# Rotary and pattern attention with four PSUM banks for scores and three for everything else, where they had three and four

## The reference, cut to what matters

```python
# rotary (L0 attn_b)
q = (layernorm(x, ...) @ Wq + bq) ; k, v = ...        # 16 heads of 16
q, k = apply_rotary(q, x), apply_rotary(k, x)
qn, kn = layernorm(q, ...), layernorm(k, ...)
att = softmax(einsum('bhqd,bhkd->bhqk', qn, kn) / sqrt(16))
a = einsum('bhqk,bhkd->bhqd', att, v);  out = a @ Wo + bo
# pattern (inside L1 attn_a)
p_probs = softmax(einsum('bhqd,bhkd->bhqk', pq, pk) * 16 ** -0.5)
pattern_out = (p_probs @ pv) @ sp_o_w.T
```

## Time and profile before

| | |
|---|---|
| median of 3 runs | 4378.23 us (4376.72 to 4392.27) |
| the profiled execution | 4388.44 us, its span 4386.7 us |
| TensorE busy | 3812.8 us (87% of the span) |
| VectorE, ScalarE, GpSimd busy | 58%, 39%, 31% |
| mean granted TensorE clock | 0.933 |

### The profile page before, as it was taken

How to read it: one execution, slowest core, us unless ns; L and a number is a source line. 1 busy time by engine, 2 the same in 40 slices (tenths; PEclk the granted TensorE clock), 3 DMA queues, 4 the chain that set the end, 5 groups by cost and what they waited for, 6 DMA issues and landing times. The chain is left out here.

```text
span 4386.7 us, 45573 instructions
## 1 busy us (share of the span) xinstructions
PE 3812.8 (87%) x16352; PEld 2470.1 (56%) x16352; DVE 2547.1 (58%) x4291; ACT 1716.1 (39%) x2934; POOL 1356.8 (31%) x1074
## 2 busy tenths in 40 slices
PE   5879888887988886999998988999888888889999
PEld 3657644445754443555555546788744444367887
DVE  5655456664456665767676756433466776564333
ACT  2423255653235552333333323222256656532222
POOL 3224312213321104333333324444322221144442
PEclk8989989998989987999999998999989999989999
DMA  2000000001000002000010111000000000010000
GB/s 75 1 22 21 14 1 1 1 1 43 17 6 6 5 22 77 25 20 25 19 26 17 27 34 38 26 26 19 19 1 1 1 1 1 6 42 22 26 9 20
DMA packets 32909, 83.35 MB, mean 19 GB/s; under 512 B 6320, under 2 KB 7472, under 8 KB 32304
## 3 DMA queue, kind: packets, MB, share of 16 engines
q1 hardware_dynamic: 32688, 80.44, 6.1%
HBM read 59.44 MB, written 4.19 MB: 15 GB/s over the span
## 5 line engine op out<-in xcount | busy, mean ns | idle before, releaser
L1175 DVE TENSOR_REDUCE max_cols<-ps 128x1 fp32r<-128x512 f32 x1024 | 634.7, 681 | 219.6 <-PE ps L1105 218.7
L1150 ACT ACTIVATE probs<-ps 128x512 f32<-128x512 f32 x1024 | 549.9, 606 | 262.1 <-PE ps L1114 173.4
L768 POOL TENSOR_TENSOR h_lo<-h,h_hi 128x512 fp32r<-128x512 f32 x304 | 392.1, 1290 | 819.2 <-ACT h_hi L853 819.2
L932 DVE TENSOR_TENSOR gated<-silu,ps 128x512 f32<-128x512 f32 x288 | 198.1, 688 | 680.6 <-PE ps L235 656.5
L847 ACT ACTIVATE silu<-ps 128x512 f32<-128x512 f32 x304 | 181.6, 598 | 896.8 <-PE ps L235 896.7
L233 PE MATMUL ps<-xn_hi,w_hi 128*128 128x512 f32 x1216 | 483.1, 397 | 0.0
L234 PE MATMUL ps<-xn_lo,w_hi 128*128 128x512 f32 x1216 | 476.9, 392 | 0.0
L235 PE MATMUL ps<-xn_hi,w_lo 128*128 128x512 f32 x1216 | 476.3, 392 | 0.0
L338 POOL CAST o_hi<-o_scaled 128x512 fp32r<-128x512 f32 x64 | 39.0, 610 | 869.2 <-DVE o_scaled L1197 869.2
L1120 PE MATMUL ps<-probs,v_aug 128*32 128x512 f32 x2048 | 294.9, 650 | 0.5 <-ACT probs L1150 0.5
L1105 PE MATMUL ps<-k_alone,q_stack 128*128 128x512 f32 x512 | 215.4, 444 | 53.8 <-DVE max_cols L1175 24.9
(11 more groups left out here) (462 smaller groups left out, 7842.7 us busy)
## 6 DMA issues: line engine op xcount, KB each, us to landing
raw<-in_w_ffn SPq DMA_DIRECT2D x76, 448.0 KB, 3.2
raw<-raw SPq DMA_DIRECT2D x256, 64.0 KB, 2.0
composed_inputs<-in_m_latent SPq DMA_DIRECT2D x2, 2560.0 KB, 9.4
raw<-in_w_mamba SPq DMA_DIRECT2D x8, 448.0 KB, 5.8
raw<-in_w_latent SPq DMA_DIRECT2D x5, 448.0 KB, 6.3
x<-in_x SPq DMA_DIRECT2D x4, 512.0 KB, 6.7
gated_pattern<-gated SPq DMA_DIRECT2D x4, 512.0 KB, 3.4
raw<-gated_pattern SPq DMA_DIRECT2D x4, 512.0 KB, 4.4
```

What stands on the lines that cost most here:

```text
L768: nc.gpsimd.tensor_tensor(HL[:, b % 3, :], hb[:, b % 2, :], HH[:, b % 3, :].bitcast(F32), ALU.subtract).then_inc(G.sem, G.step((s, ev)))
L932: nc.vector.tensor_tensor(ga if routed(i) else hb[:, i % 2, :], sg[:, i % 2, :], bank[2 + i % 2], ALU.mult).then_inc(V.sem, V.step((s, "ga ...
L1150: nc.scalar.activation(self.PB[:, n % 8, :], self.scores(n), ACT.Exp, scale=self.scale).then_inc(A.sem, A.step((s, ("exp", n))))
L1175: nc.vector.tensor_reduce(self.MB[:, self.tile_of(g, h) % 2, q, col:col + 1], self.psum(ev), op=ALU.max, axis=AX.X, negate=True).then_inc( ...
```

## The change

In rotary and pattern the scores get banks 0 to 3, all other items but `pv` share banks 4, 5 and 7, and `q_stack` gets a third buffer: the same numbers as in grouped. The list of items, their order and the sizes of all instructions stay as they are.

```diff
-                self.SCORES, self.AUXB, self.NQ = ((0, 1, 2, 3), (4, 5, 7), 3) if k_tiles else ((0, 1, 2), (3, 4, 5, 7), 2)
+                self.SCORES, self.AUXB, self.NQ = ((0, 1, 2, 3), (4, 5, 7), 3) if k_tiles else ((0, 1, 2, 3), (4, 5, 7), 2)
```

## The result

The changed kernel took 4408.78 us, the median of 8 runs (4401.44 to 4416.68), against 4383.59 us for the kernel before, the median of 8 (4376.72 to 4395.70): 1.0053 of it, with an interval of 1.0037 to 1.0069. That is 0.5% slower: 25.2 us between the medians, 23 us by the ratio. I had predicted 4387 us and a range of 4362 to 4410. The profiled execution took 4411.63 us, its span 4409.7 us.

What follows compares the result with a forecast made beforehand. No engine was full; TensorE, with the longest queue, waited for exponentials and auxiliary banks. A loss of 13.5 us less 2 x 1 and 2.5 gave 9 us on a 4378 us median: 4387 us, range 4362 to 4410.

Steps and rivals of the forecast that it cites:

- rival 1: The fourth score bank pays: half of the 44 us idle before the scores comes back, 4356 us; chance 0.13.
- rival 2: In half the groups auxiliary banks bind in full, ScalarE then late for stacks' copies; 30 us, 4408; chance 0.13.
- rival 3: The clock: a tenth more of the two stages' 776 us at the lower level, 19 us, 4406; chance 0.12.
- 0.45 us a group: Loss taken as the middle of all 30 groups that carry maxima of a next group; 13.5 us.
- second step: Pattern group: maxima matmuls wait longer for banks; pv moves from 1586.20 to 1586.8, bias 0.4 us late, taken up later.
- third step: Pattern group: bias bank wanted one maxima matmul earlier; pv 0.6 us late, not covered, reaching the next group.
- The fourth stack: Pattern group: it now waits for the copy of the first stack, so its load goes 0.3 us late.
- Other groups: Groups with a value projection after the bias: pv about 0.5 us late; rotary's groups estimated at 0.3 to 0.4.
- The last groups: Last group of a stage, without maxima: each of four steps gives back 0.22 us, about 1 us a stage.
- Where the fourth score bank pays: Gains: about 1 us in each stage's last group, 0.8 us in each of three rotary groups fetching another function table.
- 0.88, or within 0.02 of 0.91: Granted clock in rotary and pattern: forecast stays at 0.91 within 0.02; a fall to 0.88 would mean rival 3.
- same: Whole kernel's time within about 0.5% (22 us), what a measurement can tell from no change; chance 0.71.

Runs made afterwards that it cites:

- e1: Three score and three auxiliary banks in rotary and pattern (bank 3 unused), against the kernel before: 4413.24 us, ratio 1.0054.
- e4: The changed kernel once more, four score and three auxiliary banks with two query buffers, against the kernel before: 4413.38 us, ratio 1.0059.
- e2: Only a third buffer of the query stack, banks as before, against the kernel before: 4389.23 us, ratio 1.0007.
- e6: Changed kernel's four and three banks, with unread score matmuls filling TensorE's waits, against the kernel before: 4389.03 us, ratio 1.0000.
- e7: Kernel before (three score and four auxiliary banks) with unread score matmuls filling TensorE's waits, against it unfilled: 4370.44 us, ratio 0.9960.
- e9: Kernel before's banks, VectorE's normalisation moved one slot later, behind the bias addition, against the kernel before: 4412.94 us, ratio 1.0056.
- e3: Four score and three auxiliary banks and a third query buffer in rotary alone, against the kernel before: 4407.78 us, ratio 1.0042.

## Why the prediction was right or wrong

**The mechanism: right in the main.** The score bank's gain is not in the total (rival 1 falls, though PE's wait at the first bias shrank from 1.12 to 0.84 us; at the second it is 1.44 for 1.35), the auxiliary banks' waits take its place (72.1 us, forecast over 60; 2.6, forecast under 20), and e1 shows the auxiliary bank to be the whole loss. ScalarE was not late for the stacks' copies in plain groups, and the fourth step's exponentials begin at 1626.24, before PE's second bias at 1628.42, so rival 2 falls there as well.

**The size: twice what I said.** The loss is 25.2 us between the medians, 23 by the ratio, and my sum was 9. It is nearer to the prices of rivals 2 and 3 (4408 and 4406 us) than to the forecast. The stated range holds it by 1.2 us, and that is luck: the same program, measured again as e4, took 4413.38 us, outside of it. The term "0.45 us a group" and the one for the groups with a table load were mis-sized, and the clock had none, as follows.

What the prediction says of a third buffer of `q_stack` is about something that the change doesn't have; no number hangs on it.

**The steps in a pattern group.** In the group of the earlier trace rows, which begins at 1608.17 in the changed kernel, the loads are:

```profile
1612.75 0.18 PEld L1105 LDWEIGHTS ps<-k_stack,q_stack 64*128 64x128 f32 x1 [0.82 <-ACT probs L1150]
...
1613.80 0.16 PEld L1120 LDWEIGHTS ps<-probs,v_aug 128*32 128x32 f32 x8 [0.24 <-issue]
1614.79 0.52 PEld L1110 LDWEIGHTS ps<-h_pattern_hi,max_cols 128*128 128x128 f32 x4 [0.84 <-DVE max_cols L1175]
...
1618.02 0.28 PEld L1105 LDWEIGHTS ps<-k_stack,q_stack 64*128 64x128 f32 x1 [2.11 <-ACT probs L1150]
...
1619.34 0.20 PEld L1120 LDWEIGHTS ps<-probs,v_aug 128*32 128x32 f32 x8 [0.44 <-issue]
```

Counted from each group's start (1581.03 before), the second step's `pv` is 0.46 us late (I said 0.6) and the bias 0.18 (0.4). In the third step m11 stands 2.11 us for the bias bank with s3 behind it, and `pv` is 0.64 us late (0.6). The fourth stack is 0.3 us late, as forecast. The first step gains 0.14 us, where I had nothing.

Only a group without time at 1.2 GHz in either kernel shows what such delays cost. Pattern's group 7 is one (0 and 0.1 us); it starts at 1461.72 and 1484.54. Third step, before and then changed:

```profile
1473.64 0.22 PEld L1105 LDWEIGHTS ps<-k_stack,q_stack 64*128 64x128 f32 x2 [1.65 <-ACT probs L1150]
1473.75 0.19 PEld L1114 LDWEIGHTS ps<-q_stack,k_stack 64*128 64x128 f32 x1
1474.30 0.16 PEld L1120 LDWEIGHTS ps<-probs,v_aug 128*32 128x32 f32 x8 [0.36 <-issue]
```

```profile
1496.57 0.22 PEld L1105 LDWEIGHTS ps<-k_stack,q_stack 64*128 64x128 f32 x2 [1.56 <-ACT probs L1150]
...
1497.60 0.16 PEld L1120 LDWEIGHTS ps<-probs,v_aug 128*32 128x32 f32 x8 [0.24 <-issue]
```

This is the group with a value projection after the bias: m10 meets the bank, s2 and m11 come behind it, and `pv` is at 13.06 us instead of 12.58. That is the 0.5 us of the step "Other groups", and the group is 0.58 us longer (22.0 for 21.4). Three other groups ran wholly at 2.4 GHz in some run of either split: pattern's group 11 (21.6 in e2, 22.0 in e4), its group 8 (23.9 in the kernel before and 23.8 in e2, 24.7 in e4) and rotary's group 12 (20.5 in e2, 21.4 here). So the four lose 0.4 to 0.9 us from the waits alone, where I took 0.45 as the middle of all.

**The last groups: right.** Their steps come 2.39 to 2.47 us apart (2.60 before), and the final twelve exponentials are one unbroken run:

```profile
1015.48 6.19 ACT L1150 ACTIVATE probs<-ps 128x512 f32<-128x512 f32 x12
```

Rotary's last group is 1.7 us shorter and pattern's 1.4; I gave 1 each.

**The groups with a table load: wrong.** The step "Where the fourth score bank pays" gave them 0.8 us each. Of rotary's three (groups 0, 4 and 8), group 0 gained more, 2.0 us (28.73 to 26.70). But group 8 is 3.3 us longer (25.98 to 29.25) and group 4 is 3.6, and in e1, with three score banks, they are as long (29.2 and 29.3), so this is the auxiliary bank's. The timeline around the last stack of group 8 shows why, before and then changed:

```profile
842.37 0.68 DVE L1181 TENSOR_TENSOR q_stack<-q_stack,ps 128x512 fp32r<-128x512 f32 x1
...
843.17 0.28 PEld L1101 LDWEIGHTS ps<-heads_hi,h_rotary_hi 128*128 128x128 f32 x1 [0.23 <-issue]
...
844.15 0.18 PEld L1114 LDWEIGHTS ps<-q_stack,k_stack 64*128 64x128 f32 x2 [0.36 <-issue]
```

```profile
858.49 0.68 DVE L1181 TENSOR_TENSOR q_stack<-q_stack,ps 128x512 fp32r<-128x512 f32 x1
...
859.29 0.19 PEld L1101 LDWEIGHTS ps<-heads_hi,h_rotary_hi 128*128 128x128 f32 x1 [2.69 <-issue]
...
860.86 0.68 ACT L1135 ACTIVATE k_stack<-ps,c 128x512 fp32r<-128x512 f32 x1
861.65 0.29 PEld L1101 LDWEIGHTS ps<-heads_hi,h_rotary_hi 128*128 128x128 f32 x1 [2.06 <-issue]
...
862.80 0.29 PEld L1114 LDWEIGHTS ps<-q_stack,k_stack 64*128 64x128 f32 x2 [0.65 <-ACT k_stack L1135]
```

With four banks the fourth stack waits for the bias addition; with three it waits for the copy of the first stack, and ScalarE comes to that copy only after the layer norm's work: the stack goes 861.65 - 833.55 = 28.10 us into the group, not 843.17 - 818.17 = 25.00. I had costed this wait in pattern alone, at 0.3 us, where the copy comes at once. It is the last part of rival 2, a late copy that the fourth stack waits for, with another reason. In the same group m6 meets a bank that `mean` had taken (it goes 6.49 us into the group in place of 5.09), and that step's `pv` is 0.77 us late, a wait that my pattern group doesn't have.

**The clock: a term that was missing, of open size.** My sum had no term for it and left it to rival 3, at 19 us and a chance of 0.12. The two stages spend 170.7 us at 1.2 GHz and spent 138.9. What a microsecond there costs is an estimate. e2 and before run the same instructions in rotary, 13.8 us apart at the lower level and 6.4 in length, 0.46 for one. The two ends of one set of runs of the kernel before, 4374.80 us at a mean of 0.937 and 4397.62 at 0.931, give 0.43 (22.8 us for 53), but a straight line through all 62 runs that stand beside the experiments gives 0.27. So the 31.8 us more cost 9 to 14 us by these prices. Twelve matmuls of the output projection show it in the group of the earlier trace rows: from the third step's `pv` to the next score they take 1625.71 - 1619.34 = 6.37 us and took 1596.98 - 1591.56 = 5.42; with the waits filled (e6) it is 1597.41 - 1593.41 = 4.00.

```profile
1593.41 0.16 PEld L1146 LDWEIGHTS ps<-probs,v_aug 128*32 128x32 f32 x8 [0.24 <-issue]
...
1597.41 0.18 PEld L1140 LDWEIGHTS ps<-q_stack,k_stack 64*128 64x128 f32 x1 [0.36 <-issue]
```

The account of the profiled stages is then +25.4 = 9 to 14 for the clock - 3 in the last groups + 14 to 19 over the other 30. The last number is a remainder; I had 13.5 less 2.5. By the filled pair, e6 against e7, it is 10.6 = 3 - 3 + 11, with the fillers' unequal cost in it.

**What stays open** is the size of the clock's part. By the profiled executions filling takes 15 of the 25.4 us that part the two kernels. By the medians it takes only 0.13 of the 0.53%, some 6 us: e6 over e7 is still 1.0040. Beside intervals of 0.10 to 0.16% either way that is not clear of nothing. e6's profiled run was the fastest of its twelve (4377.04 us, clock 0.946, the others 0.940 to 0.944). And over the whole execution the changed kernel's clock isn't lower: its eight runs have a mean of 0.933, the 62 of the kernel before 0.933 as well. In the profiled pair the rest of the execution spent 18.2 us less at 1.2 GHz and was 2.4 us shorter. So no run shows by itself that the clock had a part in the 23 us; in the two stages it is 0 to 15 us by these figures, and the order of the waits has the rest, where my sum said 9. My sign that would refute, "0.88, or within 0.02 of 0.91", was too coarse: 0.02 over 776 us is 31 us at the lower level, 8 to 14 us of time, as much as the whole forecast or more.

Of the 22 us by which the median was missed, 16 are the loss and 5 the base: three runs had given 4378 us, all eight gave 4383.59, and later ones 4386 to 4390. With 0.53% the measurement just leaves the "same" to which I gave 0.71.

## What to carry to other kernels

Where two sets of buffers share one memory, follow what the smaller set waits for in every kind of group, those with a stage's own projections and table loads first: here four groups without time at 1.2 GHz lost 0.4 to 0.9 us each, near the forecast, and two with a table load over 3 us instead of gaining. Where the granted clock moves too, a wait moved on TensorE may be priced twice, as the wait itself and as the clock of the matmuls behind it; the runs here put the second price at 0.3 to 0.45 us for one at the lower level, and filling, which costs time itself, brought back 0.18. Compare groups that ran wholly at one level first, since they give the price of the wait by itself. And before an instruction is moved to shorten a wait, ask what waits for the instructions that now come later: e9 took 1.6 us out of TensorE's wait, gained 0.95 in a group without an output projection, and lost by those with one.

## What the runs showed of the hardware

More work made the kernel faster: 165 unread matmuls in either stage, placed in waits of over a microsecond, raised the granted clock of pattern from 0.91 to 0.99, and e7 takes 0.9960 [0.9945, 0.9975] of the kernel before. The last group of pattern, with the same matmuls and the same three score banks, ran wholly at 2.4 GHz in the kernel before (10.5 us) and wholly at 1.2 in e2, e3 and e9 (15.1 us). In e2 even the list of instructions ahead of it is that of before, so the list doesn't fix the level. The Trainium skill (TensorE: Matmul & The Clock Gate, "A second HAM failure mode: psum-queue depth-cycling") says that TensorE's short idle times between PSUM banks keep its clock going up and down; the runs agree, with 20.1 us more at the lower level in rotary when the auxiliary set lost its fourth bank (e1), though two profiles of the same banks (before and e2) lie 13.8 us apart there.
